# Masking and adding the gelu on GpSimd instead of VectorE, with a few pieces of the order moved

## What is computed

```python
x = layernorm(x + L0_attn(x))       # linear attention by a 256x256 matrix, in float32
x = layernorm(x + L0_ffn(x))        # 8 experts, softmax gate with a threshold
x = layernorm(x + L1_attn(x))       # 16 heads; each row attends among its own heads
# last part: 768 of the 1024 rows of a batch are replaced by their gelu
scores = x @ w_router
_, top_idx = top_k(scores, 768)                     # highest scores
out = x.at[batch, top_idx].set(gelu(x[top_idx] @ w_block))
x = layernorm(x + out)
```

## Time and profile before

| | |
|---|---|
| time, median of three runs | 1335.28 us (1333.78 to 1336.28) |
| the profiled execution, its own time | 1334.37 us |
| its span, first to last instruction | 1332.6 us |
| mean granted TensorE clock | 0.895 of full speed |
| TensorE / VectorE / ScalarE / GpSimd busy | 88% / 71% / 57% / 39% of the span |

### The profile page before, as it was taken

The page is one execution under the profiler, slowest core; times in us unless marked ns, Lnnn a source line. Parts: engine busy times, 40 slices in busy tenths (PEclk is TensorE's granted clock), DMA queues, the critical chain, the costliest instruction groups (busy, mean ns, idle before and its releaser), DMA issues.

```text
span 1332.6 us, 30959 instructions
## 1 busy us (share of the span) xinstructions
PE 1166.4 (88%) x12264; PEld 750.0 (56%) x12264; DVE 939.5 (71%) x2132; ACT 758.2 (57%) x1151; POOL 518.9 (39%) x865
## 2 busy tenths in 40 slices
PE   6689799998989899998999989998998988898564
PEld 4444456655665547655566556755475554664452
DVE  3544568777776868768776777768687777855875
ACT  3222377347963578347773478635784477736643
POOL 2235424335334354245334353343542452351134
PEclk8689898899989998799988999799987999889556
DMA  5000050203302051201602043020512015023220
GB/s 190 16 1 16 16 181 11 81 9 118 113 2 80 17 179 45 81 1 48 190 1 81 9 135 97 2 80 17 185 39 65 1 48 175 3 65 127 64 97 32
DMA packets 91608, 90.62 MB, mean 68 GB/s; under 512 B 4038, under 2 KB 80840, under 8 KB 91208
## 3 DMA queue, kind: packets, MB, share of 16 engines
q1 hardware_dynamic: 89544, 82.35, 19.5%
q0 software_dynamic: 1920, 6.29, 1.4%
HBM read 46.68 MB, written 41.94 MB: 67 GB/s over the span
## 4 chain that ended last, share of the span: by engine, by line
PE 58%; DVE 22%; ACT 7%; issue 6%; POOL 4%; DMA 2%; DVEq 0%; SPq 0%; POOLq 0%; ACTq 0%
PE bank L1948 54%; DVE blockdiag L1508 3%; DVE keys L1594 2%; DVE stats L1338 2%; DVE gelu L1596 2%; PE bank L1958 2%; DVE x L1479 2%; POOL rs L644 2%; ACT x L956 1%; DVE ct L1307 1%; ACT part L840 1%; ACT stage L840 1%; ACT blockdiag L840 1%; DVE x L1662 1%; DVE stage L1307 1%
## 5 line engine op out<-in xcount | busy, mean ns | idle before, releaser
L1948 PE MATMUL bank<-we,at 128*128 128x512 f16 x1536 | 370.8, 398 | 1.9 <-DVE x L1479 1.9
L1948 PEld LDWEIGHTS bank<-we,at 128*128 128x128 f16 x1536 | 153.2, 102 | 186.5 <-issue 32.8
L659 POOL TENSOR_TENSOR part<-part 128x512 f32<-128x512 f32 x64 | 85.1, 1329 | 344.9 <-ACTq L982 344.9
L840 ACT ACTIVATE part<-bank,wexp 128x256 f32<-128x256 f32 x256 | 103.6, 472 | 138.1 <-PE bank L1948 83.3
L1479 DVE SCALAR_TENSOR_TENSOR x<-bank,wexp,x 128x256 f32<-128x256 f32 x256 | 122.7, 479 | 52.0 <-PE bank L1948 45.4
L1948 PE MATMUL bank<-bt,wqkv 128*128 128x512 f16 x576 | 138.9, 383 | 19.2 <-DVE stage L1307 10.8
L956 ACT ACTIVATE x<-x,nm,rs 128x256 f32<-128x256 f32 x184 | 100.2, 593 | 65.0 <-POOL nm L647 64.1
L1307 DVE TENSOR_TENSOR stage<-bank,stage 128x512 f16<-128x512 f32 x110 | 74.3, 686 | 70.6 <-ACT stage L840 70.4
L840 ACT ACTIVATE stage<-bank 128x512 f16<-128x512 f32 x110 | 64.8, 597 | 89.1 <-PE bank L1948 72.8
L640 POOL TENSOR_SCALAR nm<-mv 128x2 f32<-128x2 f32 x128 | 34.1, 267 | 196.0 <-DVE mv L1343 189.4
L1948 PE MATMUL bank<-keys,blockdiag 128*128 128x16 f16 x3072 | 96.9, 193 | 7.8 <-issue 7.1
(11 more groups left out here) (211 smaller groups left out, 2291.7 us busy)
## 6 DMA issues: line engine op xcount, KB each, us to landing
scratch_qkv<-stage SPq DMA_DIRECT2D x39, 512.0 KB, 3.5
ct<-scratch_qkv SPq DMA_DIRECT2D x28, 512.0 KB, 4.9
x_in<-in_x_dram SPq DMA_DIRECT2D x32, 256.0 KB, 2.8
keys<-scratch_qkv SPq DMA_DIRECT2D x16, 512.0 KB, 5.4
scratch_o<-stage SPq DMA_DIRECT2D x16, 512.0 KB, 3.2
bt<-scratch_o SPq DMA_DIRECT2D x16, 512.0 KB, 4.7
out_dram<-x POOLq DMA_DIRECT2D x24, 256.0 KB, 2.7
scratch_qkv<-part SPq DMA_DIRECT2D x8, 512.0 KB, 3.5
```

The lines of the kernel that those rows point to most:

```text
L659: pool.tensor_tensor(part[:, 0:2, :], part[:, 0:2, :], part[:, 2:4, :], ALU.add)\
L840: return act.activation(dst, src, ACT.Copy, scale=scale)
L1948: ins = pe.matmul(dst, lhs, rhs, start=(n == 0), stop=(n == len(terms) - 1))
```

## The change

Per full turn: VectorE no longer does the masked add of the gelu; GpSimd does it in two instructions per pair, first a product of the gelu with the mask (128 x 512, the mask broadcast along the columns), then an add to the rows. GpSimd's, ScalarE's and VectorE's orders around it move. In `ending`, for batch 6, VectorE keeps doing it. Of the masked copies of half 0, copy 5 goes from ScalarE to VectorE, and VectorE makes copies 1 to 3 before the softmax of the last quarter instead of after it. On TensorE the first expert quarter of tile 6 moves ahead, between two transposes.

```diff
@@ GpSimd
+            def b_ff(b, p):
+                pool.wait_ge(ff_read, 4 * (b + 1) + p + 1)
+                pool.sem_inc(waits_held, 1)
+                chosen = msel[:, 2 * p:2 * p + 2, None].broadcast_to([P, 2, D])
+                pool.tensor_tensor(gelu[:, :, :], gelu[:, :, :], chosen, ALU.mult).then_inc(gelu_masked, 1)
+                pool.wait_ge(gelu_masked, 4 * b + p + 1)
+                pool.wait_ge(x3_scaled, 4 * b + p + 1)
+                rows = x3[:, 2 * p:2 * p + 2, :]
+                pool.tensor_tensor(rows, rows, gelu[:, :, :], ALU.add).then_inc(gelu_used, 1)
...
                     a_sum(b, 6)
                     a_sum(b, 7)
                 if c is not None:
+                    b_ff(c, 0)
+                if b is not None:
+                    ln(b, 7, 0)
+                if c is not None:
+                    b_ff(c, 1)
                     ln(c, 4, 1)
-                if b is not None:
-                    ln(b, 7, 0)
-                if c is not None:
+                if a is not None:
+                    ln(a, 0, 0)
+                if c is not None:
+                    b_store(c, 0)
+                    b_ff(c, 2)
                     ln(c, 5, 1)
-                    b_store(c, 0)
-                if a is not None:
-                    ln(a, 0, 0)
+                if b is not None:
+                    b_copy(b, 0)
+                if a is not None:
+                    ln(a, 1, 0)
                 if c is not None:
                     b_store(c, 1)
-                if b is not None:
-                    b_copy(b, 0)
-                if a is not None:
-                    ln(a, 1, 0)
-                if c is not None:
+                    b_ff(c, 3)
                     ln(c, 6, 1)
                 if b is not None:
                     b_copy(b, 1)
                 if c is not None:
                     ln(c, 7, 1)
                     b_store(c, 2)
+                if a is not None:
+                    ln(a, 2, 0)
+                if c is not None:
                     b_store(c, 3)
                 if b is not None:
                     b_copy(b, 2)
-                if a is not None:
-                    ln(a, 2, 0)
-                if b is not None:
                     b_copy(b, 3)
                 if a is not None:
                     ln(a, 3, 0)
@@ ScalarE (in turn; the same ranges in closing and ending)
                     b_pt(c, 1)
-                    b_spreadv(c, 0, range(5, 6))
+                    b_spreadv(c, 0, range(6, 7))
                     b_s(c, 3)
-                    b_spreadv(c, 0, range(6, T))
+                    b_spreadv(c, 0, range(7, T))
                     b_pt(c, 2)
...
                     b_res(c, 1)
+                    b_res(c, 2)
+                if b is not None:
+                    b_tx(b, 1)
+                if c is not None:
                     b_ff(c, 1)
                 if b is not None:
-                    b_tx(b, 1)
-                if c is not None:
-                    b_res(c, 2)
+                    a_ln2n(b, 3)
+                    b_tx(b, 2)
+                if c is not None:
                     b_res(c, 3)
-                if c is not None:
                     b_ffn(c, 0)
-                if b is not None:
-                    b_tx(b, 2)
-                    a_ln2n(b, 3)
-                if c is not None:
-                    b_ffn(c, 1)
+                    b_ff(c, 2)
                 if b is not None:
                     b_tx(b, 3)
-                if c is not None:
-                    b_ff(c, 2)
-                if b is not None:
                     b_f(b, 0)
                     b_f(b, 1)
+                if c is not None:
+                    b_ffn(c, 1)
                 if c is not None:
                     b_ff(c, 3)
@@ VectorE
             def b_ff(b, p):
...
+                if b == NB - 2:
+                    (the waits, the two instructions of L1662 and their increment, as before)
                 dve.wait_ge(gelu_used, 4 * b + p + 1)
                 pair_stats(rows, b, 4 + p, 1)
@@ VectorE, heads
                 b_pt(c, 1)
+                b_spreadv(c, 0, range(1, 4))
                 b_s(c, 3)
-                b_spreadv(c, 0, range(1, 2))
+                b_spreadv(c, 0, range(4, 5))
                 b_ssum(c, 3)
-                b_spreadv(c, 0, range(2, 5), last=True)
+                b_spreadv(c, 0, range(5, 6), last=True)
                 b_pt(c, 2)
@@ VectorE, turn
                     b_tx(b, 0)
+                if b is not None:
+                    a_ln2(b, 3)
+                if a is not None:
+                    a_tx(a, 3)
+                if b is not None:
+                    b_tx(b, 1)
                 if c is not None:
                     b_ff(c, 0)
-                if b is not None:
-                    a_ln2(b, 3)
-                if a is not None:
-                    a_tx(a, 3)
+                if a is not None:
+                    a_ap(a, 0)
+                if b is not None:
+                    b_tx(b, 2)
                 if c is not None:
                     b_ff(c, 1)
-                if b is not None:
-                    b_tx(b, 1)
-                if a is not None:
-                    a_ap(a, 0)
-                if b is not None:
-                    b_tx(b, 2)
                 if a is not None:
                     a_ap(a, 1)
@@ TensorE, turn
                     b_tz(c, 1)
+                if b is not None:
+                    a_moe(b, 6, (0,))
+                if c is not None:
                     b_tz(c, 2)
...
                 if b is not None:
-                    a_moe(b, 6)
+                    a_moe(b, 6, (1, 2, 3))
```

More of the change, by code:

```diff
@@ L227, in build_two_layer_postln @@
         gelu_used = sem("gelu_used")
+        gelu_masked = sem("gelu_masked")
         y_ready = sem("y_ready")
@@ L754, in turn @@
                 if c is not None:
-                    ln(c, 4, 1)
+                    b_ff(c, 0)
                 if b is not None:
@@ L758, in turn @@
                 if c is not None:
-                    ln(c, 5, 1)
-                    b_store(c, 0)
+                    b_ff(c, 1)
+                    ln(c, 4, 1)
                 if a is not None:
@@ L763, in turn @@
                 if c is not None:
-                    b_store(c, 1)
+                    b_store(c, 0)
+                    b_ff(c, 2)
+                    ln(c, 5, 1)
                 if b is not None:
@@ L769, in turn @@
                 if c is not None:
+                    b_store(c, 1)
+                    b_ff(c, 3)
                     ln(c, 6, 1)
@@ L1132, in turn @@
                     b_res(c, 1)
-                    b_ff(c, 1)
+                    b_res(c, 2)
                 if b is not None:
@@ L1136, in turn @@
                 if c is not None:
-                    b_res(c, 2)
+                    b_ff(c, 1)
+                if b is not None:
+                    a_ln2n(b, 3)
+                    b_tx(b, 2)
+                if c is not None:
                     b_res(c, 3)
-                if c is not None:
                     b_ffn(c, 0)
+                    b_ff(c, 2)
                 if b is not None:
-                    b_tx(b, 2)
-                    a_ln2n(b, 3)
+                    b_tx(b, 3)
+                    b_f(b, 0)
+                    b_f(b, 1)
                 if c is not None:
                     b_ffn(c, 1)
-                if b is not None:
-                    b_tx(b, 3)
-                if c is not None:
-                    b_ff(c, 2)
-                if b is not None:
-                    b_f(b, 0)
-                    b_f(b, 1)
                 if c is not None:
@@ L1267, in ending @@
                 b_pt(b, 1)
-                b_spreadv(b, 0, range(5, 6))
+                b_spreadv(b, 0, range(6, 7))
                 b_s(b, 3)
-                b_spreadv(b, 0, range(6, T))
+                b_spreadv(b, 0, range(7, T))
                 b_pt(b, 2)
@@ L1658, in b_ff @@
                 rows = [x3_of(b)[:, 2 * p + t, :] for t in range(2)]
[L1659 to L1665, removed]
+                if b == NB - 2:
+                    dve.wait_ge(x3_scaled, 4 * b + p + 1)
+                    dve.wait_ge(ff_read, 4 * (b + 1) + p + 1)
+                    for t in range(2):
+                        ins = dve.scalar_tensor_tensor(out=rows[t], in0=gelus[t],
+                                                       scalar=msel[:, 2 * p + t:2 * p + t + 1], in1=rows[t],
+                                                       op0=ALU.mult, op1=ALU.add)
+                    ins.then_inc(gelu_used, 1)
                 dve.wait_ge(gelu_used, 4 * b + p + 1)
@@ L1771, in turn @@
                     b_tx(b, 0)
-                if c is not None:
-                    b_ff(c, 0)
                 if b is not None:
```

## The result

The changed kernel takes 1390.29 us (median of five runs, 1378.97 to 1390.59) against 1333.78 us (1328.77 to 1336.28) of the kernel before, run on the same chip. The ratio is 1.0409, interval 1.0368 to 1.0449: slower by 4%. The forecast was 1391 us.

What follows compares the result with a forecast made beforehand. TensorE (88% busy) set the pace overall, but GpSimd's queue (39% busy) bound the stretch receiving the work. Six full turns x (6.5 + 3.3 + 0.5) = 61.8, less 5.0, on 1334.4 gave 1391 us, range 1350 to 1408.

Steps and rivals of the forecast that it cites:

- The queue: On GpSimd, three passes of 2.5 us ahead of `ln(c, 6, 1)`, less 1.0 us head start: 6.5 us a turn lost.
- The stores: Behind F5, `ln(a, 2, 0)` ahead of the issue of `b_store(c, 3)` delays store, copy and `a_apn(a, 3)`: 3.3 us a turn.
- The clock: TensorE stands about 4.5 us before F4, then may run at 1.2 GHz: 0.5 us a turn lost.
- The masked copies: End of `heads`: ScalarE saves 1.9 us, less what VectorE's three copies take beyond its wait: 5.0 us gained in all.
- The quarter: TensorE's tile 6: no gain except L659 moving out of the way of `mres`, about 0.3 us, within the head start.
- The lock: VectorE instructions with two SBUF inputs or in two-port mode and GpSimd's SBUF reads block each other; `mres` took 0.64 us.
- What would show it: Signs: GpSimd gapless about 770 to 794 us, VectorE idling twice, TensorE gap 4 to 5 us before F4, turns near 163.
- The sum: Whole kernel: 1334.4 us plus six full turns x (6.5 + 3.3 + 0.5) = 61.8, less 5.0, gives 1391 us.
- The first: Rival: only GpSimd's longer queue costs, the store lands in time or statistics come early, clock holds: 1368 us; chance 0.25.
- The second: Rival: GpSimd is slowed too, passes of 3.2 us, or the clock costs 2 to 3 us: 1404 to 1418; chance 0.12.
- The third: Rival: GpSimd's longer queue is hidden, `ln(c, 6, 1)` still ends by 784.5: faster, 1322 to 1329 us; chance 0.09.
- The fourth: Rival: nothing to be seen, gains of 12 us meet a cost of 2 us a turn: 1334 us; chance 0.03.

Runs made afterwards that it cites:

- the kernel with the stores first: The changed kernel with GpSimd's last steps in the earlier order, store of pair 3 issued ahead of `ln(a, 2, 0)`, masking untouched: 1357.68 us, ratio 1.0188.
- the second profiled execution: The changed kernel run once more, unaltered, on another occasion: median 1384.17 us, ratio 1.0383, profiled span 1382.9 us.

## Why the prediction was right, point by point

- **The queue**, forecast 6.5 us a turn. F5 came 6.1 us later, 792.96 for a forecast of 793.4. A pass took 2.4 us (1.05 + 0.08 + 1.27), not 2.5; the head start was 0.7 us, not 1.0 (the queue starts with `ln(b, 7, 0)` 8.21 us after `msel`; before, with `ln(c, 4, 1)`, 8.90); and the queue itself grew by 6.8 us, from 13.26 to 20.03, though the three passes and their waits take 7.4, so 0.6 of them filled idle time. Two errors of 0.3 to 0.6 us with opposite signs.
- **The stores**, forecast 3.3. `a_apn(a, 3)` came 9.5 us later, 3.4 more than F5. Norm at 798.1 for 798.3, store at 800.0 for 800.4, copy at 803.9 for 804.2. Putting the order back returned 3.24 us.
- **The clock**, forecast 0.5 us from a wait of 4.5 us before F4. Size about right, picture right in only some turns: in this one the wait was 2.83 us, since the clock was already down at F1 (2.35 us, granted clock 0.59) and F2 and F3 took 4.26 us, inside a wait that was due anyhow. The wait of 4.3 us with a slow F4 and F5 behind it, as forecast, stood in two of six turns in one execution and three in the other. By the stretches of the kernel with the stores first such a turn costs 1.4 us, which makes 0.5 to 0.7 us a turn.
- **The masked copies**, forecast a gain of 5.0 us in all. In full turns of the changed kernel the `b_o` stretch is 1.89 us shorter and the one ahead of it 0.90 longer, where I had 1.9 and 0.98; that is 5.9 us in six turns. Alone they gave 2.5 and 3.6 us.
- **The quarter**, forecast nothing but the 0.3 us by `mres`. This term was wrong: it gains 0.75 us a turn ahead of `msel`, and nothing by `mres`.
- **The lock.** `mres` went from 0.64 to 0.17 us as its neighbour on GpSimd moved. In exchange VectorE's split of `c`, 0.41 us in the earlier trace rows, took 0.74 us under GpSimd's first product. The passes of pairs 1 to 3 kept their 1.05 and 1.27 us beside VectorE's statistics, which read one operand; the add of pair 0, which starts while that split runs, took 1.33 us. The Trainium skill's rule that I weighed (SBUF — State Buffer, section "Who interferes with whom") agrees with all of these. They moved little: VectorE's next step starts 0.77 us behind the start of the split instead of 0.62, which is 0.15 us of the missing head start.
- **What would show it.** VectorE idles 2.46 and 5.21 us in front of the two statistics, as I had written. The turn is 162.7 us for a forecast of 163. GpSimd's queue ran until 794.01 on the time of before, for a forecast of 794, and its share of the chain rose to 9%. TensorE's wait before F4 is 2.83 us in this turn, not 4 to 5.
- **The sum.** Six turns grew by 49.5 us in the profiled pair (the mean of five, 8.25, times six), where I had 61.8 less 5.5 for the copies in these turns, 56.3. The queue was 0.4 us a turn too long (2.4) and the quarter's gain was missing (4.5). The whole profiled pair differs by 44.6 us, where I had 56.8: a further 5 us net were gained outside these turns, which I did not forecast: 1.6 before the first, and 4.5 from batch 7's first wproj product to the end (41.1 us, before 45.6; 43.8 in the second profiled execution), less about 1 us lost between. The agreement of 1390.29 with 1391 is better than that of the terms, and in part luck: the same kernel gave 1384.17 us on the second occasion and 1378.97 in the profiled execution. I would call the mechanism right and the size right to some 7 to 12 us.
- **The rivals.** The first, that only the queue costs (1368 us), needed the store to land in time; the stores' order cost 3.24 us. The second needed passes of 3.2 us, or 2 to 3 us of clock. The third hung on `ln(c, 6, 1)` ending by 784.5; it ended at 790.58. The fourth fell with it.

## What to carry to other kernels

An engine with 39% busy time can be the bound of just the stretch into which work is moved: look in that stretch for the engine whose queue has no gap, and count what is put in front of each instruction that others wait for. Of the change's edits those that filled real gaps paid or cost nothing (a quarter of an expert in TensorE's wait, copies in VectorE's, pair 0 in GpSimd's idle time), though their gains did not add, and three of the four pairs did not fit into any. Issue a store whose landing someone waits for ahead of any step that itself waits, and look what other transfers go out within a microsecond of it. A median that meets its forecast is not yet a term that does: compare the stretches that an edit touches with those that it does not.

## What the runs showed of the hardware that was not expected

- A store of 256 KB issued by GpSimd landed late where SyncE issued the first of two loads of 512 KB within 0.3 us of it: 6.0 to 7.0 us after its issue in twelve turns, against 2.7 us before in five turns of six (3.5 in one), where the loads went 1.2 to 1.5 us behind it, and 3.5 to 4.6 us in the changed kernel, where they went 3 to 3.6 us ahead. That the loads are the cause was not tested alone.
- Where TensorE's clock falls in a chain of waits depends on the turn. In three profiled executions of this queue (after, twice, and with the stores first) F2 and F3 took 4.1 to 4.3 us, partly at 1.2 GHz, and F4 and F5 1.47 us each, or F2 and F3 took 2.76 us and F4 with F5 4.8 to 5.3 us; never both, and both kinds in each execution. With every product done twice and the waits before F1 and F2 longer (3.8 and 2.6 to 4.0 us), all six turns had both slow.
- GpSimd's product with a mask broadcast along the columns, 128 x 512, took 1.05 us, less than the add of two full operands, 1.27 us. Operation and broadcast differ together here; no run separates them.
